# Selective scan: a second place for the B row and a third for the products, in half of the token buffer

## What is computed

```python
dA = exp(dt[:, :, None] * A)                       # per token, channel and state
h = dA * h + (dt * u)[:, :, None] * B[:, None, :]  # runs along the tokens
y = einsum('bdn,bn->bd', h, C)                     # sum over the 16 states
y = (y + x_conv * D) * silu(z);  out = layernorm(x + y @ W_out)
```

## Time and profile before

| | |
|---|---|
| median of 3 runs | 4609.65 us (4603.08 to 4611.93) |
| the profiled execution | 4598.24 us |
| its span, first to last instruction | 4596.5 us |
| busy: PE, DVE, POOL, ACT | 79%, 73%, 39%, 29% of the span |
| mean granted clock of PE | 0.917 of 2.4 GHz |
| units in all | 512 (4 sequences of 128) |

### The profile page before, as it was taken

The page is one execution under the profiler, slowest core; times in us unless marked ns, Lnnn a source line. Parts: engine busy times, 40 slices in busy tenths (PEclk is TensorE's granted clock), DMA queues, the critical chain, the costliest instruction groups (busy, mean ns, idle before and its releaser), DMA issues. The chain is left out here.

```text
span 4596.5 us, 41097 instructions
## 1 busy us (share of the span) xinstructions
PE 3631.2 (79%) x13936; PEld 2136.1 (46%) x13936; DVE 3376.9 (73%) x5059; ACT 1314.6 (29%) x2104; POOL 1811.5 (39%) x874
## 2 busy tenths in 40 slices
PE   5799879987998799687778677777777786777779
PEld 2687569755975597532224222224222233222244
DVE  4685458645864585569997579995699976799955
ACT  3112210231022102343332343331533323433310
POOL 1101210121012101218984058881098850498910
PEclk9899889998998898889999789998999998899989
DMA  3000200020002000315652135551055531365520
GB/s 123 1 1 1 74 1 1 1 74 1 1 1 74 1 1 1 97 35 202 209 201 92 52 127 198 202 201 61 17 199 203 203 113 57 111 205 201 198 76 21
DMA packets 159071, 417.65 MB, mean 91 GB/s; under 512 B 21745, under 2 KB 58993, under 8 KB 158593
## 3 DMA queue, kind: packets, MB, share of 16 engines
q1 hardware_dynamic: 158850, 414.83, 26.5%
HBM read 388.01 MB, written 26.78 MB: 90 GB/s over the span
## 5 line engine op out<-in xcount | busy, mean ns | idle before, releaser
L1347 POOL TENSOR_TENSOR hc<-h,c_sb 128x1024 f32<-128x1024 f32 x512 | 1193.9, 2353 | 654.4 <-DVE h L1372 444.1
L1276 PE MATMUL PS<-hc,ident 128*128 128x512 f32 x2048 | 1080.5, 655 | 311.1 <-POOL hc L1347 286.5
L1276 PEld LDWEIGHTS PS<-hc,ident 128*128 128x128 f32 x2048 | 386.0, 203 | 832.9 <-POOL hc L1347 501.8
L1316 ACT ACTIVATE da<-dt,a_neg 128x1024 f32<-128x1024 f32 x384 | 437.6, 1141 | 521.0 <-DVE h L1372 521.0
L1355 DVE TENSOR_TENSOR PS<-dtu,PS 128x1024 f32<-128x1024 f32 x384 | 463.8, 1209 | 23.9 <-PE PS L1259 23.8
L1372 DVE TENSOR_TENSOR_SCAN h<-da,state,PS 128x1024 f32<-128x1024 f32 x192 | 444.0, 2333 | 0.0
L1372 DVE TENSOR_TENSOR_SCAN h<-da,PS 128x1024 f32<-128x1024 f32 x192 | 432.0, 2272 | 0.0
L100 POOL TENSOR_TENSOR ln_rstd<-ln_var,eps_pow 128x4 f32<-128x4 f32 x65 | 71.5, 1106 | 844.6 <-DVE ln_var L93 844.6
L1259 PE MATMUL PS<-bc,pick 128*128 128x512 bf16 x768 | 251.8, 414 | 148.8 <-DVE h L1372 116.1
L1338 POOL TENSOR_TENSOR bu<-bu,dtu 128x1024 f32<-128x1024 f32 x128 | 301.1, 2352 | 78.3 <-DMA bu<-bc_rows 76.5
L859 POOL TENSOR_TENSOR mix<-attn,rw 128x1024 f32<-128x1024 f32 x64 | 121.3, 1906 | 516.1 <-POOLq L736 464.8
(11 more groups left out here) (244 smaller groups left out, 6075.2 us busy)
## 6 DMA issues: line engine op xcount, KB each, us to landing
c_sb<-bc_rows SPq DMA_DIRECT2D x512, 512.0 KB, 4.0
bu<-bc_rows SPq DMA_DIRECT2D x128, 512.0 KB, 5.5
xT<-in_xT SPq DMA_DIRECT2D x16, 512.0 KB, 7.3
tok<-in_x SPq DMA_DIRECT2D x4, 2048.0 KB, 13.7
x_after_layer<-tok SPq DMA_DIRECT2D x16, 512.0 KB, 3.0
xT_after_layer<-xT SPq DMA_DIRECT2D x16, 512.0 KB, 3.9
x2T<-xT_after_layer SPq DMA_DIRECT2D x16, 512.0 KB, 6.6
tok<-x_after_layer SPq DMA_DIRECT2D x4, 2048.0 KB, 13.5
```

The source lines that it names most:

```text
L1276: op = pe.matmul(bank(Y + j), ident[:, :], hc[:, v % 2, j * CHUNK:(j + 1) * CHUNK], start=(n == 0), stop=(n == N - 1))
L1316: act.activation(decay_at(v), dt[:, m, at], ACT.Exp, scale=a_neg[:, n:n + 1]).then_inc(dr, 1)
L1347: pool.tensor_tensor(hc[:, v % 2, :], h[:, v % 3, :], c_sb[:, v % 3, :], ALU.mult).then_inc(hr, 1)
```

## The change

Half of `tok` (tiles 8 to 15) is free during the scan, because those tokens are now loaded at the start of the last block, in two transfers of 512 KB, with a semaphore each. Tiles 8 to 11 become the third place of the products, tiles 12 to 15 the second place of the B row. The waits on the places follow: load of B row p waits for the scan of pool unit p-2, the product of unit v for the gather of v-3. SP issues the load of B row p+2 where it issued that of row p+1, and two B rows ahead of the first C row.

```diff
+    LATE = TILES // 2
...
-                sp.dma_start(tok[:, :, :], x2_dram[b].rearrange("(i p) d -> p i d", p=P))\
+                sp.dma_start(tok[:, 0:LATE, :], x2_dram[b].rearrange("(i p) d -> p i d", p=P)[:, 0:LATE, :])\
                   .then_inc(sem("tok2_in"), 16)
...
+        spare = [tok[:, i:i + 4, :].rearrange("p i d -> p (i d)") for i in (LATE, LATE + 4)]
+        hc_at = [hc[:, 0, :], hc[:, 1, :], spare[0]]
+        bu_at = [bu[:, :], spare[1]]
...
+        bl = [sem(f"b_loaded{w}") for w in range(2)]
...
-                        op = pe.matmul(bank(Y + j), ident[:, :], hc[:, v % 2, j * CHUNK:(j + 1) * CHUNK],
+                        op = pe.matmul(bank(Y + j), ident[:, :], hc_at[v % 3][:, j * CHUNK:(j + 1) * CHUNK],
...
-                    if p:
-                        sp.wait_ge(sd, on_pool[p - 1] + 1)
-                    sp.dma_start(bu[:, :], bc_dram[n, where(r)[2]].partition_broadcast(P)).then_inc(bl, 16)
+                    if p >= 2:
+                        sp.wait_ge(sd, on_pool[p - 2] + 1)
+                    sp.dma_start(bu_at[p % 2], bc_dram[n, where(r)[2]].partition_broadcast(P)).then_inc(bl[p % 2], 16)
...
                     if v == 0:
                         load_b(0)
-                    elif v - 3 in on_pool[:-1]:
-                        load_b(on_pool.index(v - 3) + 1)
+                        load_b(1)
+                    elif v - 3 in on_pool[:-2]:
+                        load_b(on_pool.index(v - 3) + 2)
...
-                    pool.wait_ge(bl, 16 * (p + 1))
-                    pool.tensor_tensor(bu[:, :], bu[:, :], dtu[:, m, at], ALU.mult).then_inc(bp, 1)
+                    pool.wait_ge(bl[p % 2], 16 * (p // 2 + 1))
+                    pool.tensor_tensor(bu_at[p % 2], bu_at[p % 2], dtu[:, m, at], ALU.mult).then_inc(bp, 1)
...
-                    if v >= 2:
-                        pool.wait_ge(yr, v - 1)
-                    pool.tensor_tensor(hc[:, v % 2, :], h[:, v % 3, :], c_sb[:, v % 3, :], ALU.mult).then_inc(hr, 1)
+                    if v >= 3:
+                        pool.wait_ge(yr, v - 2)
+                    pool.tensor_tensor(hc_at[v % 3], h[:, v % 3, :], c_sb[:, v % 3, :], ALU.mult).then_inc(hr, 1)
...
+        late = {i: sem(f"tok2_late{i}") for i in (LATE, LATE + 4)}
...
                         dve.wait_ge(mm, i + 1)
+                        if i in late:
+                            dve.wait_ge(late[i], 16)
...
             def _(sp):
+                for i in (LATE, LATE + 4):
+                    sp.dma_start(tok[:, i:i + 4, :], x2_dram[b].rearrange("(i p) d -> p i d", p=P)[:, i:i + 4, :])\
+                      .then_inc(late[i], 16)
```

More of the change, by code:

```diff
@@ L1238, in state_space @@
         Y, BS = 0, 2
-        br, dr, bd, sd, sv, hr, yr, yd, bl, bp = (sem(n) for n in (
+        br, dr, bd, sd, sv, hr, yr, yd, bp = (sem(n) for n in (
             "b_spread", "decay_ready", "b_times_u", "scan_done", "state_saved", "product", "y_added", "y_taken",
-            "b_loaded", "b_times_u_pool"))
+            "b_times_u_pool"))
+        bl = [sem(f"b_loaded{w}") for w in range(2)]
         cl = [sem(f"c_loaded{w}") for w in range(3)]
@@ L1371, in scan @@
                     first = 0.0 if half == 0 else state[:, m, n:n + 1]
-                    dve.tensor_tensor_scan(h[:, v % 3, :], decay_at(v), bu[:, :] if v in on_pool else b_bank(v),
+                    dve.tensor_tensor_scan(h[:, v % 3, :], decay_at(v), bu_at[on_pool.index(v) % 2] if v in on_pool else b_bank(v),
                                            first, ALU.mult, ALU.add).then_inc(sd, 1)
```

## The result

The changed kernel takes 4541.2 us (median of 4), the one before 4610.2 us: a ratio of 0.9856, 95% interval 0.9841 to 0.9871. The same kernel in a second comparison: 0.9857 (0.9835 to 0.9880). Against 4610 us the ratio makes some 66 us; the two medians lie 69 us apart. Forecast were 50.

A forecast was written before the change was run, and what follows sets the result against it. DVE was taken as the bound, idle 45.6 us in the scan stages. Stages 43.4 plus tail 6.9 made 50.3 us, off 4609.65: about 4560 us, range 4540 to 4592 (forecast alone 4547 to 4570).

The forecast's parts named there:

- the gain inside the stages: Four scan stages: 4 x 403 = 1612 us instead of 1655.4, a gain of 43.4 us; 55.4 with no idle.
- The bound and the floor: Scan stages: DVE is the bound, with a floor of about 400 us per stage against 411.6 to 418.4 measured.
- hand-made period: One four-unit scan period of 12.1 us worked: times_u done 1.8 us before its scan starts.
- The second B place: POOL's B row load in the stages: 76.5 us of POOL waits go, and DVE's 17.7 us at times_u.
- The 3 us per stage left for the clock: Stages: DVE idle still allowed where a lower-clock gather of PE falls beside a collect.
- The rival of the clock: Stages: PE's lower clock stays and DVE still pays 18.4 + 9.3 us; 24.6 us gained, 4585 us; chance 0.14.
- The third product place: Stages: POOL's 68.9 us of waits for gathers go, unless PE falls more than a unit behind.
- The tail: Behind each stage's last scan: last collect starts at 8.0 instead of 10.9 us; 1.7 us new per stage, 6.9 us.
- Entry and tokens: First C row behind two B rows, and 1 MB of tokens loaded in the last block: cost 0 each.
- The load is hidden anyway: Rival: B load already fits into two products, so the 17.7 us stay; 32.6 us gained, 4577 us; chance 0.04.
- No change: Rival: waits move to PE, or the second place doesn't act; 4600 to 4615 us; chance 0.06.
- Slower by C rows: Rival: C loads meet B loads in the queue and POOL's period grows to 13.15 us; 4632 us; chance 0.06.

The follow-up runs named there:

- run 1: Changed kernel with the second B row place kept and the products back in two places: ratio 0.9876 to the kernel before.
- run 2: Changed kernel with the third product place kept and the B row back in one place, loaded as before: ratio 0.9962 to the kernel before.
- run 4: Kernel before, no new places, B row load issued one step sooner, in front of the C load instead of behind it: ratio 0.9873.
- run 3: Kernel before with nothing but the later load of token tiles 8 to 15: ratio 1.0006.
- runs 5 to 7: Changed kernel with an unread second transfer of 512, 256 or 128 KB in front of each C row: ratios 1.0299, 1.0280, 1.0258 to the kernel before.
- runs 9 and 10: Five pool units per round instead of four: on the changed kernel, 0.9813; on the kernel before with one B place and sooner B load, 1.0155.

## Why the prediction was right, and where its sum was off

The measured 4541.2 us lies inside the range of 4540 to 4592 us, but only just: it is 6 us below 4547, the lower end that was given for the forecast alone (all idle gone and the tail gone). The mechanism held, and one term of the sum, the gain inside the stages, was too small.

*The bound and the floor.* DVE at 400 us per stage: measured 399.8 to 400.4. The steps of the hand-made period hold to 0.2 us.

*The second B place.* Right, and larger than I had it. I gave it 17.7 us of its own and let "both parts together" take the rest. Runs 1 and 2 part them: alone it takes 53.9 us of the stages, the third place alone 9.7. So the late spreads (18.4 us) and gathers (9.3 us) were consequences of the B load too. The Trainium skill, "DMA: Bandwidth & Descriptors", section "Anatomy of one DMA", from which 3.2 us were estimated, is for another issuing path; this load landed in 5.5 us behind a C row and in 3.8 us in front of it (medians), and came near 3.2 us only at its shortest (3.5 and 3.2 us).

*The 3 us per stage left for the clock* are the term that was mis-sized; it measured 0.2 us. The lower clock did stay, at most of the gathers that had run at it: in PE's timelines of the four stages 49 gathers of some 494 took over 2.4 us before, and 38 after, where 1.9 to 2.0 us are usual. Two of the first stage after:

```profile
2290.78 3.32 PE L1282 MATMUL PS<-hc,ident 128*128 128x512 f32 x4
...
2417.23 3.75 PE L1282 MATMUL PS<-hc,ident 128*128 128x512 f32 x4 [0.66 <-DVE dt L1385]
```

None of the 38 is followed by a wait of DVE for a spread, the one beside a collect (2417.23) included: DVE's only waits of that kind are the four entries. My own sum had 0.95 us left after a slow gather and said no wait; I then left 12 us for the case beside a collect, for which I had worked out nothing. 43.4 us should have read 55.4, the end that I gave for no idle at all, and the sum 62.3, which is what stages and tails measured. The rival of the clock is right about the clock (granted 0.92 to 0.94 before, 0.94 after) and wrong about the time: the clock still falls, and nobody waits for it in the stages. The Trainium skill, "TensorE: Matmul & The Clock Gate", section "A second HAM failure mode", describes such a clock; the trace agrees that it stays.

*The third product place.* It removes POOL's waits for gathers as said, 30.8 to 0.9 us behind the B place. In the stages these cost DVE little or nothing: 1601.5 us with two product places in run 1 and 1599.1 in run 4, against 1600.0 with three. What the third place gives is in the tail: 24.3 against 27.4 and 29.5 us. In time that cannot be told: the intervals of the changed kernel (0.9841 to 0.9871 and 0.9835 to 0.9880) overlap that of run 1 (0.9860 to 0.9893), and they come from separate comparisons.

*The tail.* 6.9 us forecast, 6.9 measured, but that both are the same is partly luck: a gather there does run at the lower clock, and not the last one. PE's last gathers of the first stage after:

```profile
2457.92 3.45 PE L1282 MATMUL PS<-tok,ident 128*128 128x512 f32 x4 [2.62 <-POOL tok L1354]
2461.21 3.60 PE L1282 MATMUL PS<-hc,ident 128*128 128x512 f32 x8
```

The tails measured 5.9 to 6.3 us, not 5.7, and 7.4 to 8.4 before, not 7.4 each. The sum was 1.5 us short on both sides (22.8 against 24.3 and 29.7 against 31.2), and the difference came out right.

*Entry and tokens.* Entry: POOL waits for the first C row in four stages instead of one, and DVE for none but 0.5 us at its first pool scan; cost 0, as taken. Tokens: run 3, 0.

*The load is hidden anyway*: fallen with run 1, where the B place alone gave nearly all. *No change*: fallen with the result. *Slower by C rows*: in the changed kernel there is no such wait but one of 0.8 us; a second transfer per C row brings it about (runs 5 to 7), and nothing smaller was tried.

## What to carry to other kernels

When one engine waits for two things in turn, write out the loop that each wait closes, with the queue's order in it, and compare it with the period of the bound engine: the loop above that period is the first suspect, and here a wait taken away elsewhere mostly moved into it (run 2). Before giving a transfer more memory, see whether the issuing queue holds it behind something that it does not need. Once only the bound engine is late, the slack of the others is worth moving work to, and then more buffers can be needed (runs 9 and 10).

## What was not expected of the hardware

A second transfer in front of each C row moved the C row's median landing from 4.1 us to 7.2, 7.2 and 7.3 us with 128, 256 and 512 KB; each writes all 128 partitions. The stages differed by 7 us per stage over this fourfold size. What sets this cost was not separated further. And a mere change of place in the queue, from behind a C row to in front of it, took the B row's median landing from 5.5 to 3.8 us.
